# Eight stages of attention and feed-forward on one core: statistics moved into the tails of the stages, the weight rounding pipelined by units, and the squares of the last attention's queries folded

## The reference, cut to what matters

```
def _layernorm(x, axis=-1, eps=1e-05):
    m = jnp.mean(x, axis=axis, keepdims=True)
    v = jnp.var(x, axis=axis, keepdims=True)
    return (x - m) / jnp.sqrt(v + eps)
...
    x = x + _L0_xattn_ref(_layernorm(x, axis=-1), ctx_4096, ...)   # stage a0: 32 heads, bias and mask
    x = x + _L0_ffn_ref(_layernorm(x, axis=-1), ...)               # stage f0: a base product and gated experts
    x = x + _L1_xattn_ref(_layernorm(x, axis=-1), ctx_4096, ...)   # stage a1: patches
    x = x + _L1_ffn_ref(_layernorm(x, axis=-1), ...)               # int8 weights, computed inside stage a2
    x = x + _L2_xattn_ref(_layernorm(x, axis=-1), ctx_4096, ...)   # stage a2: 32 heads, rotary embedding
    x = x + _L2_ffn_ref(_layernorm(x, axis=-1), ...)               # stage f2: NF4-rounded weights
    x = x + _L3_xattn_ref(_layernorm(x, axis=-1), ctx_4096, ...)   # stage a3: 32 query heads, RMS norm of q and k
    x = x + _L3_ffn_ref(_layernorm(x, axis=-1), ...)               # stage f3: 64 experts, 16 chosen
```

```
        def nf4_quant_dequant(w):
            flat = w.reshape(-1, BLOCKSIZE)
            absmax = jnp.max(jnp.abs(flat), axis=1, keepdims=True)
            normalized = flat / jnp.where(absmax == 0, 1.0, absmax)
            bounds = (NF4_CODE[:-1] + NF4_CODE[1:]) * 0.5
            idx = jnp.searchsorted(bounds, normalized)
            return (NF4_CODE[idx] * absmax).reshape(shape)
```

## Time and profile before

| | |
|---|---|
| time, median of 3 runs | 3103.66 us (3102.98 to 3105.22) |
| the profiled execution | 3096.28 us, its span 3094.5 us |
| TensorE's granted clock over the span | 0.963 |
| busy over the span: PE, DVE, ACT, POOL | 2861.9, 1972.3, 1386.0, 1318.5 us |
| stages by the timeline | a0 to 904.8, f0 906.1 to 988.4, a1 from 989.5, a2 to 1857.7, f2 1859.0 to 2075.9, a3 2077.1 to 2980.0, f3 from 2981.1, store to 3094.5 |

### The profile page before, as it was taken

How to read it: one execution, slowest core, us unless ns; L and a number is a source line. 1 busy time by engine, 2 the same in 40 slices (tenths; PEclk the granted TensorE clock), 3 DMA queues, 4 the chain that set the end, 5 groups by cost and what they waited for, 6 DMA issues and landing times. The chain is left out here.

```text
span 3094.5 us, 44830 instructions
## 1 busy us (share of the span) xinstructions
PE 2861.9 (92%) x16417; PEld 2482.4 (80%) x16452; DVE 1972.3 (64%) x3494; ACT 1386.0 (45%) x3409; POOL 1318.5 (43%) x1177
## 2 busy tenths in 40 slices
PE   7999999999977896789999998989999999999967
PEld 6888888888765784678888886878999999999945
DVE  5777777778764787779888874344444444444453
ACT  3656556566531673234444432214444344443520
POOL 6455445545421754365555530013434444443430
PEclk9999999999987898999999999999999999999988
DMA  4122112212121002111111103100101000000000
GB/s 133 49 58 60 58 51 61 61 50 65 43 83 40 18 5 69 31 45 45 42 38 39 38 16 125 43 22 21 28 21 28 25 24 25 25 28 19 17 28 28
DMA packets 77816, 131.86 MB, mean 43 GB/s; under 512 B 10016, under 2 KB 23584, under 8 KB 77216
## 3 DMA queue, kind: packets, MB, share of 16 engines
q1 hardware_dynamic: 68096, 112.09, 12.2%
q10 hardware_dynamic: 9504, 16.91, 1.7%
HBM read 114.23 MB, written 14.75 MB: 42 GB/s over the span
## 5 line engine op out<-in xcount | busy, mean ns | idle before, releaser
L89 PE MATMUL a_pa<-a_wo,a_ot 128*128 128x512 f32 x2304 | 538.5, 391 | 10.3 <-issue 7.5
L89 PEld LDWEIGHTS a_pa<-a_wo,a_ot 128*128 128x128 f32 x2304 | 429.7, 188 | 105.9 <-issue 13.1
L362 DVE SCALAR_TENSOR_TENSOR a_nf_acc<-a_nf_t,a_nf_acc 128x512 f32<-128x512 bf16 (+1 forms) x462 | 403.1, 873 | 42.4 <-ACT a_nf_t L316 11.4
L316 ACT ACTIVATE a_nf_t<-a_nf_w,a_nf_shifts 128x512 bf16<-128x512 f32 (+1 forms) x495 | 321.7, 709 | 204.0 <-DVE a_nf_w L346 174.4
L89 PE MATMUL a_pa<-h_t,a_wqk 128*128 128x512 f32 x1536 | 373.1, 395 | 1.7 <-DVE h_t L773 1.7
L89 PEld LDWEIGHTS a_pa<-h_t,a_wqk 128*128 128x128 f32 x1536 | 281.8, 188 | 56.4 <-DVE h_t L773 1.9
L89 PE MATMUL a_pa<-a_wv,ctx_t 128*128 128x512 f32 x960 | 233.0, 399 | 29.1 <-POOL a_wv L532 15.5
L89 PE MATMUL a_pa<-ctx_t,a_wqk 128*128 128x512 f32 x960 | 226.8, 393 | 21.5 <-POOL a_wqk L1651 21.2
L89 PEld LDWEIGHTS a_pa<-a_wv,ctx_t 128*128 128x128 f32 x960 | 180.6, 191 | 66.8 <-issue 15.5
L89 PEld LDWEIGHTS a_pa<-ctx_t,a_wqk 128*128 128x128 f32 x960 | 181.2, 189 | 60.8 <-POOL a_wqk L1651 23.2
L1009 POOL TENSOR_TENSOR a_prob<-a_prob,a_inv 128x512 f32<-128x512 f32 x128 | 130.6, 1042 | 182.5 <-DVE a_inv L1375 182.5
(11 more groups left out here) (360 smaller groups left out, 5979.2 us busy)
## 6 DMA issues: line engine op xcount, KB each, us to landing
a_raw<-in_a_w SPq DMA_DIRECT2D x288, 256.0 KB, 2.6
a_nf_w<-in_nf ACTq DMA_DIRECT2D x32, 256.0 KB, 2.7
nf_rounded<-a_nf_acc ACTq DMA_DIRECT2D x32, 256.0 KB, 2.0
f_rows<-nf_rounded SPq DMA_DIRECT2D x22, 256.0 KB, 3.0
ctx_kept<-ctx_t SPq DMA_DIRECT2D x1, 4096.0 KB, 17.1
ctx_t<-ctx_kept SPq DMA_DIRECT2D x1, 4096.0 KB, 14.6
f_cols<-nf_rounded SPq DMA_DIRECT2D x11, 256.0 KB, 3.7
a_ctx_raw<-in_ctxt SPq DMA_DIRECT2D x4, 512.0 KB, 6.3
```

What stands on the lines that cost most here:

```text
L89: ins = nc.tensor.matmul(out, lhs(a), rhs(b), start=first and i == 0, stop=last and i == 2)
L316: self.nc.scalar.activation(self.t[:, m % NF4_RING, cols], self.w[:, p % 2, cols], ACT.Identity, bias=self.shifts[:, u - 2:u - 1], scale=s ...
L362: ins = nc.vector.scalar_tensor_tensor(acc, t, c, acc, inner, outer)
```

## The change

It has five parts.

1. `CarriedNorm`: the statistics of blocks 0 to 6, and the joined variance of blocks 0 to 3, are taken in the tail of the stage before, after each addition to x; POOL makes the factor of that half there. The next stage begins with applying block 0, takes the statistics of block 7 and the second half, and in f0 and f3 mixes the applying with the LO parts. There POOL begins its weight split once all eight blocks are applied. In a1 the loads are told apart and DVE's order is changed.
2. `Rounding.units`: units 0 and 1 of the next block stand between units 9 and 10 of the present one, `top` has two buffers, and in a0 the ring has 6 copies; ACT begins six units (four shifted copies) ahead, DVE two.
3. a2: 2 units instead of 24 ahead of the loop, 6 (3+1+2) in each of the first ten heads, then 5.
4. a3: ACT squares in two instructions of 64 partitions each, so that half the features lie beside the other half; DVE adds the two (`fold_squares`), and PE makes four products with two columns (`sides`) instead of eight with one. In every fourth head `queries(h + 2, 0)` stands ahead of the scores. Output waits for `o_taken` by half.
5. One more semaphore release (`carry.close()`) stands behind the store.

```
+class CarriedNorm(Norm):
+    def take_on_vector(self, nc, b, x):
+        nc.vector.bn_stats(self.stats[:, b, :], x[:, b, :]).then_inc(self.own, 1)
+    def half_on_vector(self, nc, dve, g):
+        bs = slice(4 * g, 4 * g + 4)
+        dve.wait_ge(self.own, 8 * g + 4)
+        for b in range(4 * g, 4 * g + 4):
+            nc.vector.bn_aggr(self.mv[:, b, :], self.stats[:, b, :]).then_inc(self.own, 1)
+        dve.wait_ge(self.own, 8 * g + 8)
+        nc.vector.tensor_scalar(self.var[:, bs], self.mv[:, bs, 1], 1e-5, None, ALU.add).then_inc(self.var_ready, 1)
+    def half_on_gpsimd(self, nc, pool, g):
+        bs = slice(4 * g, 4 * g + 4)
+        pool.wait_ge(self.half_set, 1)
+        pool.wait_ge(self.var_ready, g + 1)
+        nc.gpsimd.tensor_tensor(self.rstd[:, bs], self.var[:, bs], self.half[:, bs], ALU.pow).then_inc(self.rstd_ready, 1)
...
         dve.wait_ge(norm.rstd_ready, 1)
+        norm.apply(nc, 0, h[:, 0, :], x).then_inc(self.h_ready, 1)
+        norm.take_on_vector(nc, NB - 1, x)
+        norm.half_on_vector(nc, dve, 1)
+        for b in range(1, NB):
+            if b == 4:
+                dve.wait_ge(norm.rstd_ready, 2)
+            norm.apply(nc, b, h[:, b, :], x).then_inc(self.h_ready, 1)
+            if b >= 3:
+                low(b - 3)
+        for b in range(NB - 3, NB):
+            low(b)
...
                 nc.vector.tensor_tensor(x[:, b, :], bank(key), x[:, b, :], ALU.add).then_inc(added, 1)
+                if n == H // 2 - 1 and b > 0:
+                    dve.wait_ge(added, added_count["o", n, b - 1])
+                    ahead.take_on_vector(nc, b - 1, x)
+                    if b == 4:
+                        ahead.half_on_vector(nc, dve, 0)
...
+            p, u = (n - 2) // NF4_UNITS, (n - 2) % NF4_UNITS
+            if u < 8:
+                p, u = p, u + 2
+            elif u < 10:
+                p, u = p + 1, u - 8
...
                 if p > 0:
-                    dve.wait_ge(self.done, p)
+                    dve.wait_ge(self.v_ready, p)
+                if p > 1:
+                    dve.wait_ge(self.done, p - 1)
...
-            rounding.on_scalar(act, 2)
+            rounding.on_scalar(act, 6)
...
+            rounding.on_vector(dve, 2)
             for h in range(H):
...
-            rounding.on_scalar(act, 3 * NB)
+            rounding.on_scalar(act, 2)
...
-            rounding.on_vector(dve, 3 * NB)
+            rounding.on_vector(dve, 2)
...
-        return (2, 1, 2) if step < 14 else (2, 0, 2)
+        return (3, 1, 2) if step < 10 else (2, 1, 2)
...
             norm.on_gpsimd(pool)
+            pool.wait_ge(norm.h_ready, NB)
             for i, (w, loaded, split) in enumerate(((wa, a_loaded, a_split), (wb, b_loaded, b_split))):
...
-                pe.wait_ge(squared, 2 * head + 2)
-                for b in range(NB):
-                    ins = nc.tensor.matmul(out[:, b:b + 1], q2[:, b * P:(b + 1) * P], ones[:, :], start=True, stop=True)
+                pe.wait_ge(folded, head + 1)
+                for i in range(4):
+                    ins = nc.tensor.matmul(out[:, 2 * i:2 * i + 2], q2[:, 0, i * P:(i + 1) * P], sides[:, :],
+                                           start=True, stop=True)
...
-                nc.scalar.activation(q2[:, cols], bank(key), ACT.Square).then_inc(squared, 1)
+                for rows in range(2):
+                    nc.scalar.activation(q2[64 * half:64 * half + 64, rows, :], bank(key)[64 * rows:64 * rows + 64, :],
+                                         ACT.Square).then_inc(squared, 1)
...
+            def fold_squares(head):
+                dve.wait_ge(squared, 4 * head + 4)
+                nc.vector.tensor_tensor(q2[:, 0, :], q2[:, 0, :], q2[:, 1, :], ALU.add).then_inc(folded, 1)
```

More of the change, by code:

```diff
@@ L134, with __init__ @@
 class TransposedNorm:
-    def __init__(self, nc, st, x, ident, h_t, banks, space, h, lnw_in=None, h2=None, sq=None):
-        self.nc, self.x, self.ident, self.h_t, self.lnw_in, self.h, self.h2, self.sq = nc, x, ident, h_t, lnw_in, h, h2, sq
+    def __init__(self, nc, st, norm, x, ident, h_t, banks, h):
+        self.nc, self.x, self.ident, self.h_t, self.h = nc, x, ident, h_t, h
         self.tp = [bank.rearrange("p (c n) -> p c n", c=DC) for bank in banks]
[L144 to L153, removed]
@@ L254, with __init__ @@
     SCALE = 2.0 ** 60
-    def __init__(self, nc, st, at, flat_in, rounded, first, sizes):
+    def __init__(self, nc, st, at, flat_in, rounded, first, sizes, early, ring):
         code = np.array(NF4_CODE, np.float32)
@@ L264, in __init__ @@
         self.nc, self.flat_in, self.rounded, self.first, self.sizes = nc, flat_in, rounded, first, sizes
+        self.early, self.ring = early, ring
         blocks = max(sizes)
@@ L321, in on_vector @@
         nc = self.nc
-        for unit in range(self.dve_at, min(self.dve_at + count, len(self.sizes) * NF4_UNITS)):
-            p, u = unit // NF4_UNITS, unit % NF4_UNITS
+        for p, u in self.units(self.dve_at, count):
             cols, blocks = slice(0, self.width(p)), self.sizes[p]
@@ L1185, in _ @@
                 transpose_weights(h, 1)
+                if h % 4 == 3 and h + 2 < H:
+                    queries(h + 2, 0)
                 if h + 1 < H:
@@ L2878, in _ @@
         def _(pool):
-            norm.set_half(nc)
-            norm.rstd_on_gpsimd(nc, pool)
+            norm.half_on_gpsimd(nc, pool, 1)
+            ahead.half_on_gpsimd(nc, pool, 0)
         @block.tensor
@@ L3017, in add, with rest_of_h @@
                 nc.vector.tensor_tensor(x[:, b, :], pd[:, d % 2, :], x[:, b, :], ALU.add).then_inc(d_used, 1)
-            norm.stats_on_vector(nc, Steps(dve, norm_own), x)
-            turn(0, range(3))
-            dve.wait_ge(norm.rstd_ready, 1)
-            for b in range(NB):
-                norm.apply(nc, b, norm_h[:, b, :], x).then_inc(h_ready, 1)
-            for b in range(NB):
+                if group == FF_GROUPS - 1 and b > 0:
+                    dve.wait_ge(d_used, d)
+                    ahead.take_on_vector(nc, b - 1, x)
+                    if b == 4:
+                        ahead.half_on_vector(nc, dve, 0)
+            def rest_of_h(b):
                 dve.wait_ge(h_hi, b + 1)
```

285 lines of the change are left out of this document (148 added, 137 removed).

## The result

The changed kernel takes 3025.55 us (median; 3103.32 before in the same comparison). The ratio is 0.975, with a 95% interval from 0.9731 to 0.9769: 2.5% faster, 78 us. One further execution took 3634 us with a granted clock of 0.741 and is left out as disturbed. A second pairing, run with the experiments, gave 3028.6 against 3098.28, ratio 0.9775 (0.9761 to 0.9788). The profiled execution has a span of 3023.6 us against 3094.5, 70.9 less. Single executions of one kernel lie up to 9 us apart here (3095.27 to 3104.46 of the kernel before in one comparison), so parts of a few us are read from the stages' times in the trace and not from medians.

A forecast was written before the change was run, and what follows sets the result against it. TensorE was taken as the bound in the long heads, so only fewer matmuls or less TensorE idling pay. Gains less losses summed to 67.0 us; from 3103.66 that gives 3036.7, forecast as 3036, range 3022 to 3061.

The forecast's parts named there:

- Rounding in a0: a0's heads: normalised weights written seven folds earlier, so TensorE's waits for late key copies shrink; +18 us, bounds 8 to 24.
- ring minus lead: a0's rounding: still two copies, so ScalarE is no more patient when VectorE is late, and only 8 us might come.
- Tails: Stage ends: added statistics delay the last additions; -3.0 us for a0, a2 and a3 together, -0.6 for f0, -3.3 for f2.
- The last release: End of the kernel: one more semaphore release costs a barrier, -1.3 us.
- Start of f0: First side product 13.85 us after the stage's start instead of 20.05, the cast waiting for GpSimd's base split; +6.2 us.
- The rival that GpSimd's power holds VectorE: f0's start, also f3, f2, a3: the power blocks VectorE's applies; 8 us less gain, about 3044; chance 0.2.
- Start of f3: Router product at 21.9 us instead of 29.4 behind GpSimd's weight steps, +7.5; at 15 to 17 if small instructions slip through.
- Squares in a3: a3's heads: four products instead of eight save 8 TensorE records of 0.106 us a head; +26.5 us.
- the two prices of the Trainium skill: a3's halved products: 25 ns each by issue gap, giving 6.4 us, or 107 ns by weight load, which the rows support.
- the fold: Before a3's loop, VectorE's addition of the squares' halves stands ahead of the first queries' LO part: -0.7 us.
- The exchange of queries and scores: a3, eight heads: the keys' wait goes, but scores wait 0.7 us for ScalarE instead; gain nothing.
- a2: Wait ahead of the heads falls from 21.24 to 2.3 us, with clock +21; one more unit in ten heads costs 4.

The follow-up runs named there:

- 4: Changed kernel with a ring of 4 shifted copies in a0 and ScalarE two copies ahead, early units kept: 3027.37 us.
- 5: Changed kernel with a0's rounding as before: units in plain order, ring of 4, ScalarE two units ahead of the loop: 3046.6 us.
- experiment 10: Changed kernel with no statistics in f2's tail, all eight taken at a3's start: 3027.59 us.
- experiment 3: Changed kernel with a3's queries and scores in the old order in every fourth head too: 3026.67 us.
- experiment 2: Changed kernel with ScalarE's two copies of the values ahead of the two output copies, in three of four heads of a3: 3021.97 us.
- 1: Changed kernel with a3's squares as before (one square of 128 partitions, no fold, eight products with a column of ones): 3040.33 us.
- experiment 9: Changed kernel with a2's rounding placed as before, 24 units ahead of the heads, then 5 and 4 in each: 3042.69 us.

## Why the prediction was right, and where not

The forecast (3036, range 3022 to 3061) held the time. Its sum of 67 was 4 short in the profiled executions and 11 short by the medians of the same comparison (77.8; 69.7 in the second). Errors of 13 us cancelled in it; the steps fare as follows.

*Rounding in a0*: mechanism right, size too small. The early units are the whole of it (4, 5). The prediction took 16 of 20.5 us of waits and the clock of one gap. The keys' wait lost 15.8, the 2.7 us in three waits for VectorE's additions to x went as well, and so 18.5 of the 24.8 us of the heads (the tail's first addition came at 894.55, now 869.73) are waits. The other 6 fit the granted clock, which had been priced at 1.9: by hundreds of us from 100 on it was 0.98 and 0.93 in two stretches before, and only in the last, short one below 1.00 after (0.98 up to the tail). In all it stood at half for 17.1 us before and 3.4 after. That share was not tested by itself, and in the changed kernel's second profile a0 took 2.3 us more, with 13.6 us at half. Its argument that ring minus lead is unchanged was true and didn't matter.

*Tails*: a0's cost 0.7 (1.0), f2's 3.0 (3.3, and 2.7 by experiment 10). The last release (-1.3) can't be read: from f3's router product to the end are 83.9 us before and 83.9 to 86.4 in the changed kernels.

*Start of f0*: mechanism right, and the product came 1.2 us earlier than taken. 1.0 of that is the base weight's transfer, which landed 9.3 us behind the stage's start and not 10.3, so that the copy that holds the cast ended earlier. The chain was 1.2 us shorter too (applies follow one another at 0.48 and not 0.54, an apply and a LO part take 1.05 and not 1.23), but the cast waited that out. The rival that GpSimd's power holds VectorE is refuted by the rows above: three applies in 1.45 us, begun 0.5 us ahead of the power of 1.32 and ended inside it. The Trainium skill ("SBUF — State Buffer", Who interferes with whom) has GpSimd and VectorE exclude one another for a whole instruction where VectorE's is in a two-port mode, or has two inputs in SBUF while GpSimd's reads it. For the weight steps the trace agrees (a cast of 4.19 and a two-input subtraction of 1.80 us above), for the power it doesn't.

*Start of f3*: the step that failed is "the second at 16.8, and the two subtractions, which read two inputs in SBUF, at 21.4". The order of holds was right, and two executions show nearly it (20.65), but usually one hold fewer is met: 16.2, which the prediction had as its other end. By the same section of the Trainium skill whoever issues first gets the ports. The same four instructions do meet three holds in experiment 3 and two in the changed kernel; but where the two part, GpSimd's step and the keys' cast begin at 2933.66 both in the one and at 2936.69 and 2936.70 in the other, so the records don't show who was first.

*Squares in a3*: the step that failed is "ScalarE gets two more squares a head ... both well under half busy". Their price of 0.85 us a head for PE's records was right (experiment 2: 0.89 and 0.91), and of the two prices of the Trainium skill ("TensorE: Matmul & The Clock Gate", Back-to-back issue gap, and LDWEIGHTS) the second holds: 0.106 us a record. But 16 records had covered a chain that the prediction didn't look at: PE's last product with the values, ScalarE's copy of the output (0.60), its copy of the values, which frees the bank that PE needs next: 1.22 us from the first record of the squares to the next product in the rows above. The busy share of ScalarE said nothing of that. It took 0.3 us a head, some 10 us. Ahead of the loop the fold was priced at 0.7; behind a3's start the first squares came 1.5 later than with it undone, and the second 2.3 (1). The exchange of queries and scores, priced at nothing, cost 3.3 (3).

*a2*: the wait went from 21.24 to 2.24 (2.3 predicted), the heads lost 4.1 (4, by experiment 9). In a1 the first product came 1.7 earlier and the mask's transfer took that back, as the prediction had it. The gain up to the end of the wait was 17.5 and not 19.0, because 1.6 us were lost between a1's first scores and the wait; why stays open.

## What to carry to other kernels

Before halving the work of a bottleneck engine, list what its old time covered: the next wait is found by asking which buffer it takes next and which instruction of which queue frees it, not by the busy shares. Where a stall sits at a hand-over in a queue (normalised weights behind a block's end), moving the producer's step earlier was worth 24 us here, while deeper rings were worth nothing. Small VectorE instructions belong ahead of GpSimd's long steps on SBUF, and statistics only into tails whose bottleneck leaves room for them.

## What the runs showed of the hardware that was not expected

A short pause can cost the clock or not. a2's wait of 2.24 us was the same in the changed kernel and in experiment 3; in the first the 24 products behind it took 5.73 us, in the second

```profile
1269.52 7.32 PE L89 MATMUL a_pa<-ctx_t,a_wqk 128*128 128x512 f32 x24 [2.24 <-POOL a_wqk L1677]
```

and a2 from the wait to f2's start took 543.4 us instead of 539.9. The profiles of the changed kernels with a2 unchanged fall on these two (539.2 to 540.0 in nine, 543.3 to 543.4 in three), and the granted clock tells them apart: between 1240 and 1360 us it stood at half for 3.4 us in the first profile and for 13.6 in that of experiment 3, from the end of the wait on. So 3.7 us of any single comparison here may be the clock. What decides between the two is not shown.
